# A fused cross-attention and mixture-of-experts kernel: queries one turn further ahead, query reads first in SyncE's turn, keys and first weights split differently in the opening, the two layer norms on other engines

## The reference, cut to what matters

```
x = x + attn(layernorm(x), ctx)       # softmax(q k^T / 4 - slope_h * |j - i - (154 - 1024)|) v, then Wo, bo
x = x + moe(layernorm(x))             # 8 experts, hidden 1024, softmax gate, top 2, weights renormalised
# each expert: gelu(x @ W1[e] + b1[e]) @ W2[e] + b2[e]
```

## Time and profile before

| | |
|---|---|
| median of 3 runs | 510.2 us (507.28 to 512.9) |
| the profiled execution | 508.91 us, span 507.1 us, mean granted TensorE clock 0.922 |
| busy, share of the span | PE 83%, PEld 65%, DVE 62%, ACT 46%, POOL 44% |
| first part | to 249.67 us, then the last scatter lands and the experts start at 257.80 us |

### The profile page before, as it was taken

The page is one execution under the profiler, slowest core; times in us unless marked ns, Lnnn a source line. Parts: engine busy times, 40 slices in busy tenths (PEclk is TensorE's granted clock), DMA queues, the critical chain, the costliest instruction groups (busy, mean ns, idle before and its releaser), DMA issues. The chain is left out here.

```text
span 507.1 us, 16158 instructions
## 1 busy us (share of the span) xinstructions
PE 419.6 (83%) x5137; PEld 330.3 (65%) x5138; DVE 312.6 (62%) x875; ACT 232.4 (46%) x607; POOL 223.7 (44%) x305
## 2 busy tenths in 40 slices
PE   5565768897888999995179899989989998999981
PEld 2554556676666778873168677668867876777760
DVE  5357848796778777554526466636664765566560
ACT  1333636564555564563234444534543553445430
POOL 3123528887888886677602222222222232122232
PEclk9865979898989999998579999989998999999997
DMA  6574455555646535333322223113222322122110
GB/s 225 134 229 150 139 152 189 175 175 192 215 136 185 165 123 163 122 123 127 127 64 37 39 41 53 35 29 45 46 44 31 53 38 43 34 43 47 22 12 0
DMA packets 52967, 50.70 MB, mean 100 GB/s; under 512 B 22672, under 2 KB 47024, under 8 KB 52784
## 3 DMA queue, kind: packets, MB, share of 16 engines
q1 hardware_dynamic: 45192, 41.07, 27.0%
q0 software_dynamic: 7152, 8.47, 9.9%
q10 hardware_dynamic: 576, 0.53, 0.3%
HBM read 33.73 MB, written 17.50 MB: 101 GB/s over the span
## 5 line engine op out<-in xcount | busy, mean ns | idle before, releaser
L976 PE MATMUL ps<-area,wts 128*128 128x128 f16 (+1 forms) x2896 | 197.0, 243 | 0.1
L976 PEld LDWEIGHTS ps<-area,wts 128*128 (+1 forms) x2896 | 157.5, 103 | 41.0 <-issue 2.1
L976 PE MATMUL ps<-wts,area 128*128 x624 | 153.4, 330 | 2.2 <-DVE area L934 1.8
L718 ACT ACTIVATE area<-ps,late 128x128 f32<-128x128 f32 x312 | 89.2, 368 | 115.0 <-PE ps L976 115.0
L932 DVE TENSOR_SCALAR area<-area 128x512 f16<-128x512 f32 x78 | 33.0, 424 | 77.8 <-ACT area L718 77.7
L976 PE MATMUL ps<-area 128*128 128x154 f16 (+2 forms) x928 | 71.0, 236 | 12.0 <-DMA area<-qd 11.1
L976 PEld LDWEIGHTS ps<-area 128*128 128x128 f16 (+1 forms) x928 | 59.8, 107 | 21.2 <-issue 8.1
L595 POOL DMA_INDIRECT out<-o,row_id x20 | 31.6, 1579 | 95.1 <-issue 65.0
L595 POOL DMA_INDIRECT out<-xn,row_id x19 | 30.0, 1579 | 92.4 <-issue 79.8
L804 DVE TENSOR_REDUCE mx<-ps 128x3 f32<-128x462 f32 (+1 forms) x96 | 53.1, 579 | 24.3 <-PE ps L976 23.9
L621 ACT ACTIVATE area<-ps 128x512 f32<-128x512 f32 x80 | 47.3, 595 | 27.7 <-PE ps L976 25.5
(11 more groups left out here) (121 smaller groups left out, 419.1 us busy)
## 6 DMA issues: line engine op xcount, KB each, us to landing
stage<-in_w SPq DMA_DIRECT2D x32, 512.0 KB, 5.0
area<-xlist SPq DMA_DIRECT2D x39, 130.0 KB, 2.0
area<-qd SPq DMA_DIRECT2D x16, 256.0 KB, 2.7
qd<-wts SPq DMA_DIRECT2D x48, 64.0 KB, 1.9
area<-in_x SPq DMA_DIRECT2D x16, 128.0 KB, 2.3
out<-area SPq DMA_DIRECT2D x16, 128.0 KB, 1.8
xlist<-pad_rows SPq DMA_DIRECT2D x11, 130.0 KB, 2.5
area<-in_b SPq DMA_DIRECT2D x1, 1024.0 KB, 5.0
```

The source lines that it names most:

```text
L718: last = nc.scalar.activation(h32[par][:, c * P:(c + 1) * P], h_ps[par][m][:, f * P:(f + 1) * P], ACT.Gelu_apprx_tanh, bias=b1T[:, ds(e * ...
L976: return nc.tensor.matmul(out_, lhsT, rhs, start=start, stop=stop, skip_group_check=skip)
```

## The change

What it does, part by part:

1. `stages`: f1 = i+5, f2 = i+4; the rest stays. 21 turns, from -3. SP's turn begins with `read_q(i+3)`, the tile written a turn ago; `read_m(i+1)` stands behind `write_q`, then weights, then `load_x` (one tile further ahead), then `write_m`.
2. First norm: DVE keeps L734 and L737. POOL makes variance plus epsilon, power, and shift = -mean*rstd (three [128,1] operations). ACT makes `xn` with one Identity activation, scale and bias from these, behind the fourth and fifth exp.
3. Second norm: POOL makes variance plus epsilon and power, DVE makes `xn2` (tensor_scalar) in the next turn, between maxima groups 1 and 2. The negated maximum of the logits moves from DVE to POOL (`least`).
4. Scores: heads in pairs, one matmul of 314 columns for both heads of a pair where a group has both: 10 matmuls a tile in place of 16 (the kink's extra ones stay). `bo` is added by one matmul with two rows in place of two matmuls.
5. Opening: keys batch by batch (`pack_a` in two pieces), bias rows written by ACT's DMA queue; `values` in turn -2; no weight unit before turn -2 (one for turn -1, then two a turn, one in turn 7, none in 15, two in 16); `pack_o` and two constants are loaded in SP's turn -1 behind two weight units; `bo_split` has three operations. In turns 16 and 17 DVE's weight splits stand at the end.

```
-            return [i + n if 0 <= i + n < NT else None for n in (4, 3, 2, 0, -1, -2)]
+            return [i + n if 0 <= i + n < NT else None for n in (5, 4, 2, 0, -1, -2)]
...
+            count = lambda j: 1 if j in (-1, 7) else 2 if 0 <= j < 15 or j == 16 else 0
+            first = sum(count(j) for j in range(-1, i))
+            return list(range(first, first + count(i)))
...
+            sp.dma_start(a_sb[:, 0:A_ONE], pack_a[:, 0:A_ONE]).then_inc(s.a_in0, 16)
             load_x(0)
-            sp.dma_start(a_sb, pack_a).then_inc(s.a_in, 16)
...
+            write_k(0)
+            write_q(0)
+            read_k(0)
+            read_q(0)
+            write_k(1)
+            read_k(1)
             def turn(i):          # SP
                 f1, f2, sc, mt, b1, b2 = stages(i)
-                if 0 <= i + 1 < NT:
-                    read_m(i + 1)
+                if i > -3 and i + 3 < NT:
+                    read_q(i + 3)
+                if i == -1:
+                    read_m(0)
                 if b2 is not None:
                     store(b2)
-                if 4 <= i + 5 < NT:
-                    load_x(i + 5)
-                if f2 is not None and f2 > 0:
+                if f2 is not None:
                     write_q(f2)
-                    read_q(f2)
-                for u in weight_units(i + 1) if i > -3 else []:
+                if 0 <= i < NT - 1:
+                    read_m(i + 1)
+                for u in weight_units(i + 1):
                     load_w(u)
+                if i == -1:
+                    sp.dma_start(late[:], pack_o).then_inc(s.o_in, 16)
+                    sp.dma_start(c16[:], c16_in).then_inc(s.c16_in, 16)
+                    sp.dma_start(ids[:], ids_in).then_inc(s.c16_in, 16)
+                if i == 2:
+                    sp.dma_start(kinks[:], kink_in).then_inc(s.kink_in, 16)
+                if -1 <= i < NT - 6:
+                    load_x(i + 6)
                 if sc is not None:
                     write_m(sc)
...
+            def rstd1(t):         # POOL
+                pool.wait_ge(s.mv1_d, t + 1)
+                wait(pool, s.xn_d, t)
+                pool.tensor_scalar(rs1[:, 0:1], mv1[:, 1:2], EPS, 1.0, ALU.add, ALU.mult).then_inc(s.ve1_d, 1)
+                pool.wait_ge(s.ve1_d, t + 1)
+                pool.tensor_tensor(rs1[:, 1:2], rs1[:, 0:1], c32[:, C_HALF:C_HALF + 1], ALU.pow).then_inc(s.rstd1, 1)
                 pool.wait_ge(s.rstd1, t + 1)
-                wait(pool, s.xnT_ps, t)
-                pool.tensor_scalar(xn, xr[:, t % 8, :], mv1[:, 0:1], rs1[:, 1:2], ALU.subtract, ALU.mult).then_inc(s.xn_d, 1)
+                pool.tensor_scalar(rs1[:, 2:3], mv1[:, 0:1], rs1[:, 1:2], -1.0, ALU.mult, ALU.mult).then_inc(s.shift1, 1)
...
+            def rstd2(t):         # POOL
+                pool.wait_ge(s.mv2_d, t + 1)
+                wait(pool, s.xn2_d, t)
+                pool.tensor_scalar(rs2[:, 0:1], mv2[:, 1:2], EPS, 1.0 / (SX * SX), ALU.add, ALU.mult).then_inc(s.ve2_d, 1)
+                pool.wait_ge(s.ve2_d, t + 1)
+                pool.tensor_tensor(rs2[:, 1:2], rs2[:, 0:1], c32[:, C_HALF:C_HALF + 1], ALU.pow).then_inc(s.rstd2, 1)
...
+            def normed2(t):       # DVE
+                dve.wait_ge(s.rstd2, t + 1)
+                wait(dve, s.x2T_ps, t)
+                wait(dve, s.xs_hi, t)
+                wait(dve, s.xs_lo, t)
+                dve.tensor_scalar(xn2[:], xr[:, t % 8, :], mv2[:, 0:1], rs2[:, 1:2], ALU.subtract, ALU.mult).then_inc(s.xn2_d, 1)
...
                 if b2 is not None:   # POOL's turn
                     rows_lo(b2, b2 % 2)
+                    least(b2)
                     chosen(b2)
                 if f1 is not None:
-                    normed1(f1)
+                    rstd1(f1)
                 if b2 is not None:
                     weights_of(b2, b2 % 2)
                 if b1 is not None:
-                    normed2(b1)
+                    rstd2(b1)
...
+                if f1 is not None:   # ACT's turn, behind exps(mt, 4)
+                    normed1(f1)
                 for u in units[1:2]:
                     split_w_hi(u)
+                if i == -2:
+                    values()
...
+                nc.scalar.activation(xn, xr[:, t % 8, :], ACT.Identity, bias=rs1[:, 2:3], scale=rs1[:, 1:2]).then_inc(s.xn_d, 1)
...
                 if sc is not None:   # DVE's turn
-                    for g in range(3):
-                        maxima(sc, g)
+                    maxima(sc, 0)
+                    maxima(sc, 1)
+                if b2 is not None:
+                    normed2(b2)
+                if sc is not None:
+                    maxima(sc, 2)
...
+                while at_ < end:     # PE's scores
+                    p, hh = at_ // 2, at_ % 2
+                    both = hh == 0 and at_ + 1 < end
+                    width = KW + NK if both else NK
+                    dst = bank[:, (at_ - first) * KW:(at_ - first) * KW + width]
+                    last = mm(dst, qs[:, slot, p, :], kk[:, b, p, hh * KW:hh * KW + width], True, kink is None, True)
...
-                    for z in range(2):
-                        last = mm(misc[:, D:2 * D], c16[0:1, H_SMALL:H_SMALL + P], bo_hl[:, z, :], False, z == 1)
-                    last.then_inc(s.pr_ps, 1)
+                    mm(misc[:, D:2 * D], c16[0:2, H_SMALL:H_SMALL + P], bo_hl[:], False, True).then_inc(s.pr_ps, 1)
```

More of the change, by code:

```diff
@@ L130, in by_key @@
     def by_key(keys):
-        return keys.reshape(B, -1, DC, P).transpose(3, 2, 0, 1).reshape(P, -1)
+        return keys.reshape(B, -1, DC, P).transpose(3, 0, 2, 1).reshape(P, -1)
     ext, last = np.zeros((B, EXT, D), np.float32), np.zeros((B, P, D), np.float32)
@@ L187, in program @@
         b1T = late[:, O_B1:O_B1 + E * FC]
-        bo_row = late[0:1, O_BO:O_BO + D]
+        bo_row = late[0:2, O_BO:O_BO + D]
         area = sb("area", [P, 11616], f32)
@@ L832, in turn @@
                     dve.wait_ge(s.m8_d, b2 + 1)
-                    dve.tensor_scalar(small[:, 0:1], m8[:, 0:1], -1.0, None, ALU.mult).then_inc(s.nm_d, 1)
                     wait(dve, s.tail_d, 3 * b2)
@@ L842, in turn @@
                     maxima(sc, 3)
-                if f1 is not None and f1 > 0:
+                if f1 is not None:
                     norm1(f1)
-                for u in earlier[1:2]:
+                for u in earlier[1:2] if i < NT else []:
                     split_w_lo(u)
@@ L848, in turn @@
                     maxima(sc, 4)
-                for u in units[0:1]:
+                for u in units[0:1] if i < NT else []:
                     split_w_lo(u)
@@ L873, in turn @@
                     dve.transpose(nbT[:, sc % 2, :], nb16[:]).then_inc(s.nbT_d, 1)
-                if i == -3:
+                for u in earlier[1:2] + units[0:1] if i >= NT else []:
+                    split_w_lo(u)
+                if i == -2:
                     values()
@@ L1036, in scores @@
                 first, n = GROUPS[g]
-                for j in range(n):
-                    hh, p = (first + j) // NP, (first + j) % NP
-                    dst = ps[:, seq % 3, j * KW:j * KW + NK]
-                    last = mm(dst, qs[:, slot, p, :], kk[:, b, p, hh * KW:hh * KW + NK], True, kink is None, True)
+                end, bank = first + n, ps[:, seq % 3, :]
+                at_ = first
+                while at_ < end:
[4 more added lines that the diff above has]
+                    last = mm(dst, qs[:, slot, p, :], kk[:, b, p, hh * KW:hh * KW + width], True, kink is None, True)
                     if kink is not None:
                         keys = kinks[:, kink * N_KEYS:kink * N_KEYS + NK]
-                        for m in ((0, 1), (2,))[hh]:
-                            last = mm(dst, diagonal(p, m), keys, False, m > 0, True)
+                        for h in range(at_, at_ + 1 + both):
+                            dst = bank[:, (h - first) * KW:(h - first) * KW + NK]
+                            for m in ((0, 1), (2,))[h % 2]:
+                                last = mm(dst, diagonal(p, m), keys, False, m > 0, True)
+                    at_ += 1 + both
                 last.then_inc(s.s_ps, 1)
```

210 lines of the change are left out of this document (105 added, 105 removed).

## The result

| | before | after | ratio (95% interval) |
|---|---|---|---|
| first comparison | 509.1 us | 491.7 us | 0.964 (0.958 to 0.971) |
| beside later experiments | 505.2 us | 486.5 us | 0.962 (0.957 to 0.967) |
| profiled execution, span | 507.1 us | 490.3 us, later 481.4 us | |

The account below looks back on a forecast made before the run. POOL's two norms and queue tail, then PE, then DVE bound the turn. Savings of 9.2 (opening), 13.7 (steady), 2.4 (kink) and 3.2 (tail), 28.5 in all, gave 480.4, plus 1.3: 481.7 us; range 476 to 487, 8 in 10 472 to 496.

Parts of the forecast that it names:

- Steady turns: Turns 3 to 9: each would take 9.9 us, with DVE late next after POOL, saving 13.7 us.
- less 0.45 for what it loses: DVE's steady turn: 10.3 us with the gaps, less 0.45 for the three small operations removed, giving 9.9 us.
- Turn 5, where `xn2` was in time, took 9.94, so I take 9.9: Steady turns: before's turn 5, at 9.94 us, taken as the model for turns of 9.9 us.
- The read of turn 6 that came late is in it too: write and read now lie a turn apart.: Steady turns: the query read 2.19 us late in turn 6 would go, counted within the 9.9 us.
- the 6 us that I priced in the rival: Rival, queries still come late: turns 2 and 6 keep 3.64 + 2.19 us and the dips, 488 us; chance 0.07.
- Small operations of POOL at 0.19 us: POOL's steady turn: four added one-column operations at 0.19 us each, leaving POOL at 7.6 us a turn.
- the rival built on it: VectorE and GpSimd block each other: four small POOL operations 0.9 us longer each, turns 11.2 us, 491 us; chance 0.12.
- Opening, 9.2 forecast: Turns up to turn 3: first scores at 19.5, shorter waits, a shorter turn 2, less added waits; saves 9.2 us.
- the `pack_o` wait: Opening, end of turn -1: `bo_split` on DVE waits for the later-issued `pack_o`, adding 4.5 us (0 to 8).
- the opening's rival: The opening gives nothing: `values` at half clock and the `pack_o` wait at 8, 490 us; chance 0.15.
- Kink turns and tail, 5.6 forecast: Turns 10 to 13 save 2.4 us of PE idling; turns 14 to 17 save 3.2 us through shorter chains.
- Slower: Rival: DVE stands at `xn2` for GpSimd's power, maxima queued behind; held 4.5 us a turn gives 524 us; chance 0.04.

Follow-up runs that it names:

- s1: Kernel after with all norm operations, large and small, and the minus of the largest logit where they were before: 500.1 us, ratio to before 0.990.
- e1: Kernel after with both norms' large operations back on POOL, the small ones left where the change put them: 507.8 us, ratio to before 1.002.
- r3: Kernel after, unchanged, run and profiled again: 486.5 us, ratio to before 0.962.
- e2: Kernel after with queries made one turn less ahead and read right behind their writing, ahead of the maxima: 484.6 us, ratio to before 0.954.
- s2: Kernel after with queries one turn less ahead and SP's order of before, but x one tile further ahead: 513.4 us, ratio to before 1.014.
- e3: Kernel after with scores not paired, each head's scores a matmul of its own: 485.2 us, ratio to before 0.956.
- r2: Kernel after with the first norm's large operation alone back on POOL: 493.5 us, ratio to before 0.975.
- s4: Kernel after with its query depth kept but SP's order of before, x one tile further ahead: 498.9 us, ratio to before 0.982.

## Why the prediction was right, and where not

- **What bounds.** POOL's norms did hold the turn: putting them back as they were costs 14 us (s1), and some 20 with the new small operations still on POOL (e1).
- **Steady turns, forecast 9.9, measured 10.83 and 10.27.** This is the mis-sized term: 13.7 forecast, 7.2 and 11.2 saved. DVE is late next, as forecast. The term of the sum that failed is "less 0.45 for what it loses". The run from the reciprocal to the next turn's maxima, 7.83 us in the prediction, takes 7.78 in turns 5 and 6 of the second profile, not 7.4: the three small operations overlapped their neighbours and had held the run up by some 0.26 us only, and one maxima operation inside it now has three heads (0.63 us) where it had two (0.47). The other 2.54 us to the next reciprocal have 0.25 us of waiting for PE in them; together that is the 10.3 that I had before I took off the 0.45. Second profile, timeline of DVE, turns 6 and 7:

```profile
104.15 0.26 DVE L862 RECIPROCAL rec<-ps 128x16 f32<-128x16 f32 x1 [0.25 <-PE ps L1165]
...
111.93 1.19 DVE L842 TENSOR_REDUCE mx<-ps 128x3 f32<-128x462 f32 x2
...
114.46 0.26 DVE L862 RECIPROCAL rec<-ps 128x16 f32<-128x16 f32 x1 [0.25 <-PE ps L1165]
```

  Before, timeline of DVE, turn 3, one of the three small operations (L739) between its neighbours:

```profile
87.17 0.18 DVE L737 BATCH_NORM_AGGREGATE mv<-st 128x2 f32<-128x6 f32 x1
87.39 0.15 DVE L739 TENSOR_SCALAR rs<-mv 128x1 f32<-128x1 f32 x1
87.46 1.22 DVE L788 SCALAR_TENSOR_TENSOR wts<-stage,wts 128x1024 f16<-128x1024 f32 x1
```

  Without it, the split starts 0.10 us behind the aggregate (117.32 and 117.42 below) where it had started 0.29 behind. The step that hid it is "Turn 5, where `xn2` was in time, took 9.94, so I take 9.9". That turn had DVE busy 8.77 us with 24 instructions; turns 3 and 6 have 9.4 to 9.5 with 29 or 30. It had both its weight splits, but its end came before DVE's last operations, which fell into turn 6. From reciprocal to reciprocal DVE took 10.82 us or more in every one of before's turns 3 to 9. `xn2` on DVE takes 0.41 us, not 0.35, and on ACT `xn` takes 0.60, not 0.41; the latter is covered. The rest of the first profile's 10.83 is the waits that r3 is free of, and turn 5's clock.
- **"The read of turn 6 that came late is in it too: write and read now lie a turn apart."** Right in result, wrong in reason: in e2 they lie in one turn again and nothing is lost, so the order on SP does it. It is worth more than the 6 us that I priced in the rival: s2, with the wait for the store in it, lost 27. I had priced the old wait in the old pace.
- **Small operations of POOL at 0.19 us.** The first norm's epsilon and shift take 1.07 and 1.00 us (medians) beside DVE's splits. Second profile, timeline of POOL and of DVE, turn 7:

```profile
117.59 1.07 POOL L525 TENSOR_SCALAR rs<-mv 128x1 f32<-128x1 f32 x1 [0.57 <-DVE mv L765]
118.75 0.58 POOL L527 TENSOR_TENSOR rs<-rs,c 128x1 f32<-128x1 f32 x1
119.43 1.00 POOL L529 TENSOR_SCALAR rs<-mv,rs 128x1 f32<-128x1 f32 x1
```
```profile
117.42 1.19 DVE L826 SCALAR_TENSOR_TENSOR wts<-stage,wts 128x1024 f16<-128x1024 f32 x1
118.53 0.63 DVE L842 TENSOR_REDUCE mx<-ps 128x3 f32<-128x462 f32 x1
119.08 1.21 DVE L826 SCALAR_TENSOR_TENSOR wts<-stage,wts 128x1024 f16<-128x1024 f32 x1
```

  Each ends within 0.15 us of the split that it began in. That fits the rule that I quoted from the Trainium skill (SBUF — State Buffer, Who interferes with whom), since a split has two inputs in SBUF; and it is the rival built on it, at half its size: two operations 0.8 us longer each, not four by 0.9. POOL is at 8.4 us, not 7.6. ACT waited some 0.6 us a turn for the shift; PE's `xn` was in time, so I take it that the turn paid nothing. No run tests this.
- **Opening, 9.2 forecast, 9.25 and 9.98 measured,** by other parts than listed. First scores started at 22.95 and 22.67, not 19.5; but the `pack_o` wait of 3.8 us on DVE reached PE as 1.0 us (2.1 in the second profile), not 4.5. The granted clock in the third and fourth slice was 0.8 and 0.5, against 0.6 and 0.5, and `values` took 6.2 and 5.4 us, between the 4.9 that I took and the 9.8 of the rival, so the opening's rival came only in small part. The page of the first profile:

```profile
PEclk9785999999999999995598999899989998999996
```

  Neither depth, order (s2), norms (s1) nor pairing (e3), taken back one at a time, brings the old opening back; what is left in all these runs is part 5, lighter and split loads. No run took part 5 back, so this is by elimination.
- **Kink turns and tail, 5.6 forecast, 1.3 and 3.4 measured.** In turns 12 and 13 of the first profile PE waits 0.8 us for `xn2`, behind maxima of kink scores on DVE. In the tail, at 223.16, DVE stands 0.99 us for POOL's power before `xn2`, and PE's wait of 3.13 us for `xn2` there has this in it (the same 0.99 us on DVE in the second profile).
- **Slower.** Its mechanism, DVE held by POOL's power, is real (r2: 0.91 us a turn with 1.0 us more on POOL ahead of the power) and absent from after's steady turns by nearly nothing: in turn 7 of the first profile the power ends at 115.61 and `xn2` starts at 115.65. In the tail it came once (0.99 us, above). The rival's 524 us do not follow from its own sum: if 3.5 us a turn eat 28.5, that is some eight turns, and one us more in each gives about 518.
- **Experts** took 251.7 and 249.6 us where they had taken 250.7; the change does nothing there.

## What to carry to other kernels

When an engine is relieved, work out again whether every transfer still fits into the shorter turn: the queue that stood 12 us in seven turns of before for a landing stood 32 us in six of s2, under nearly the same order. In a queue issued in order, put what the next turn reads first ahead of whatever waits for a landing, a reused buffer's store included; depth covered less here. Take a comparison turn only after counting its instructions on the engine that you expect to be the bound. And take a small operation off a sum only by what it adds from start to start, not by its duration.

## What the runs showed of the hardware

- TensorE's granted clock fell behind waits: in e1, s2 and s4 turns with one wait of 2.1 to 6.5 us had a mean of 0.69 to 0.87 (between the levels of 1.2 and 2.4 GHz), and PE was busy 1.5 to 4 us longer for the same matmuls. With waits up to 1.2 us in each turn (r2) it stayed at 1.00. It is no strict rule: turn 5 of the first profile had 0.86 with no wait above 0.9 us, and s1 had both 1.00 and 0.86 in turns with a wait of 1.64 us.
- Two executions of one program had steady turns of 10.83 and 10.27 us on the same instructions. In the slower one DVE waited up to 0.9 us a turn for PE's logits, where it waited 0.2 in the faster. SP's issue of the spare rows (`pad_rows`) took 1.2 to 1.9 us in some turns and 0.4 in others, but in both profiles, so it is not shown to be the cause. The cause stays open.
